# Attention in front of a mixture of experts: another order within the attention steps, and part of the first head norm on GpSimd

## The reference

```python
# x: 4 sequences of 512 tokens, 512 wide; 16 heads of 32
h = layernorm(x)
q, k, v = split(h @ w_qkv)
q, k = layernorm_per_head(rope(q)) * s + b, layernorm_per_head(rope(k)) * s + b
a = tril((q @ k.T) ** 4)
x = x + ((a / a.sum(-1)) @ v) @ w_out
h = layernorm(x)
# 16 experts in 4 groups, 2 groups and 4 experts kept; a shared expert
w, sel = route(sigmoid(h @ gate.T) + bias)
x = x + sum_over_sel(w * expert_sel(h)) + shared(h)
```

## Time and profile before

| what | us |
|---|---|
| three timed runs | 1215.68, 1217.14, 1225.99 |
| their median | 1217.14 |
| the profiled execution, its own time | 1209.58 |
| its span in the trace | 1207.6 |
| first scores of sequence 0 | 88.9 |
| sequences 0 to 3 start | 88.9, 207.7, 357.1, 496.8 |
| attention ends | 609.8 |
| PE, DVE, ACT, POOL busy over the span | 958.4, 756.9, 563.6, 529.1 |

### The profile page before, as it was taken

How to read it: one execution, slowest core, us unless ns; L and a number is a source line. 1 busy time by engine, 2 the same in 40 slices (tenths; PEclk the granted TensorE clock), 3 DMA queues, 4 the chain that set the end, 5 groups by cost and what they waited for, 6 DMA issues and landing times. The chain is left out here.

```text
span 1207.6 us, 21002 instructions
## 1 busy us (share of the span) xinstructions
PE 958.4 (79%) x5770; PEld 455.7 (38%) x5771; DVE 756.9 (63%) x1663; ACT 563.6 (47%) x1009; POOL 529.1 (44%) x738
## 2 busy tenths in 40 slices
PE   5967789869777785984777799888888798878883
PEld 2432333324333332341343454444344344434441
DVE  2857865867888588849648665554455544545552
ACT  2347874866537665577235234333333233333330
POOL 0005663544415545367302003555555555555553
PEclk9988999888879887976868899899999989999996
DMA  8002333433323333655346896777777777778874
GB/s 330 13 35 93 118 105 137 140 119 112 107 88 100 137 107 110 236 204 192 107 148 207 304 319 184 193 185 184 174 188 191 178 179 181 190 174 193 183 187 78
DMA packets 76648, 193.48 MB, mean 160 GB/s; under 512 B 9904, under 2 KB 11056, under 8 KB 75312
## 3 DMA queue, kind: packets, MB, share of 16 engines
q1 hardware_dynamic: 58672, 149.53, 35.9%
q0 software_dynamic: 17920, 43.26, 19.6%
HBM read 131.67 MB, written 61.10 MB: 160 GB/s over the span
## 5 line engine op out<-in xcount | busy, mean ns | idle before, releaser
L743 PE MATMUL bank<-arena,xgT 128*128 (+1 forms) x1152 | 288.0, 387 | 3.6 <-ACT xgT L1029 3.1
L1065 POOL TENSOR_TENSOR s_p<-s_p,c_causal 128x128 f32<-128x128 f32 x256 | 153.8, 624 | 304.3 <-DVE s_p L1420 282.7
L485 PE MATMUL bank<-arena 128*128 128x512 f32 x384 | 196.5, 663 | 43.8 <-ACT arena L856 14.6
L1022 ACT ACTIVATE hT<-bank 128x512 f16<-128x512 f16 x96 | 57.3, 597 | 273.1 <-PE bank L753 273.1
L743 PEld LDWEIGHTS bank<-arena,xgT 128*128 128x128 f16 x1152 | 109.2, 100 | 133.1 <-issue 45.4
L1073 POOL TENSOR_TENSOR arena<-arena 128x768 f16<-128x768 f32 x68 | 113.0, 1662 | 87.8 <-ACT arena L821 87.7
L1109 POOL DMA_INDIRECT out<-yy,sidx x80 | 128.6, 1608 | 46.1 <-issue 44.6
L764 PE MATMUL bank<-wd,hT 128*128 128x512 f16 x576 | 146.0, 391 | 0.7 <-ACT hT L1022 0.7
L910 ACT ACTIVATE arena<-bank 128x512 f32<-128x512 f32 (+3 forms) x256 | 100.8, 439 | 93.2 <-PE bank L533 92.6
L1694 DVE TENSOR_SCALAR yy<-bank,hsc 128x512 f32<-128x512 f32 x80 | 60.0, 750 | 122.8 <-DMA out<-yy,sidx 116.6
L1029 ACT ACTIVATE xgT<-bank 128x1024 f16<-128x1024 f16 x96 | 98.2, 1023 | 78.7 <-PE bank L734 77.4
(11 more groups left out here) (172 smaller groups left out, 1390.2 us busy)
## 6 DMA issues: line engine op xcount, KB each, us to landing
wd<-w_scratch SPq DMA_DIRECT2D x82, 512.0 KB, 4.2
arena<-w_experts SPq DMA_DIRECT2D x34, 768.0 KB, 6.0
w_scratch<-arena SPq DMA_DIRECT2D x34, 768.0 KB, 4.5
arena<-w_scratch SPq DMA_DIRECT2D x17, 1024.0 KB, 7.7
xin<-x SPq DMA_DIRECT2D x4, 1024.0 KB, 5.5
arena<-x SPq DMA_DIRECT2D x4, 1024.0 KB, 4.8
x_scratch<-arena SPq DMA_DIRECT2D x4, 1024.0 KB, 5.2
xg<-xn_scratch SPq DMA_DIRECT2D x16, 256.0 KB, 4.5
```

The costliest lines, as they stand in the source:

```text
L485: mm = pe.matmul(bk[:], xnT[:, c, m * P:m * P + P], wqkv[:, c, w * E:w * E + E], start=(c == 0), stop=(c == EC - 1))
L743: mm = pe.matmul(bank[2 + k][:], xgT[:, k, xh * EC + c, :], w, start=(c == 0 and xh + wh == 0), stop=(c == EC - 1 and xh == 1))
L1065: pool.tensor_tensor(d, d, C["causal"][:], ALU.mult).then_inc(p4_masked, 1)
```

## The change

- q/k/v stage of the first sequence: the temporaries of rope exist twice there (the second pair lies in `s_sq`), and DVE ropes block m before the variance of block m - 1. DVE stops at the reciprocal (new semaphore `rstd_known`); Pool makes the product into `qkn` and, for blocks 0 to 2, the low halves. PE and ACT have the stage written out in a new order, and the next sequence's transposes and first q and k stand ahead of the last block's transposes. The weight load is split into q/k and v (`wv_in`).
- Sequences 0 to 2: at p = 0 PE does the old group's `values` ahead of v; ACT does both casts of `qkT` at the end of the p = 3 step, the four squares together, then `copy_v` and `head_squares`; its other copies move from the head of a step to the end of the one before. DVE's `finish` moves from the head of the p = 1 step to behind the fourth powers of the p = 0 step. At i = 15 `choice_places` stands ahead of `centre`. SP stores the normed rows one expert piece earlier.
- Sequence 3: `finish` likewise; the logits come in two halves at steps 5 and 6, and the choice starts a step later, `compare` and `expert_choice` then sharing a step.

```diff
-        t1, t2 = (t12[:, 2 * i:2 * i + 2, :].rearrange("p j n -> p (j n)") for i in range(2))
+        roped = [[a[:, 2 * i:2 * i + 2, :].rearrange("p j n -> p (j n)") for i in range(2)] for a in (t12, s_sq)]
+        temps = lambda b, m: roped[m % 2 if b == 0 else 0]
...
+        rstd_known, wv_in = sem("rstd_known"), sem("wv_in")
...
-            sp.dma_start(wqkv, w_qkv).then_inc(wqkv_in, 16)
+            sp.dma_start(wqkv[:, :, 0:2 * E], w_qkv[:, :, 0:2 * E]).then_inc(wqkv_in, 16)
+            sp.dma_start(wqkv[:, :, 2 * E:3 * E], w_qkv[:, :, 2 * E:3 * E]).then_inc(wv_in, 16)
...
-                halves_of(b, 0, 2)
+                halves_of(b, 0, 1)
                 if b:
                     sp.wait_ge(xn16_ready, b)
                     sp.dma_start(xn_dram[N * (b - 1):N * b, 0:E].rearrange("(m p) e -> p m e", p=P),
                                  xn16[(b - 1) % 2].rearrange("p m h e -> p m (h e)").bitcast(I32)).then_inc(xn2_out, 16)
-                halves_of(b, 2, 4)
+                halves_of(b, 1, 4)
...
-                elif i == 5:
-                    for m in range(MB):
+                elif i in (5, 6):
+                    pe.wait_ge(x2T_sb, upto(pb, 3))
+                    for m in (2 * i - 10, 2 * i - 9):
                         logits(pb, m, bkA)
...
                     scores(b, i)
+                    if i and i % MB == 0:
+                        values(b, i - 1)
                     if b + 1 < B:
                         fill(b, i)
-                    if i:
+                    if i % MB:
                         values(b, i - 1)
...
+            def first_qk(m):
                 for w, (done, read) in enumerate(((q_ps, q_roped), (k_ps, k_roped))):
                     if m:
                         pe.wait_ge(read, upto(0, m - 1))
                     qkv(0, m, w, bank[w], done)
+
+            def first_v(m):
                 if m:
-                    if m >= 2:
-                        pe.wait_ge(qkT_sb, 2 * upto(0, m - 2))
-                    qk_transposes(0, m - 1, bank[6], bank[7])
                     pe.wait_ge(v_sb, upto(0, m - 1))
+                else:
+                    pe.wait_ge(wv_in, 16)
                 qkv(0, m, 2, bank[2], v_ps)
-            for m in range(MB):
-                pe.wait_ge(xT_sb, upto(0, m + 2) if m < 2 else upto(1, m - 2))
-                first_T(1, m, bank[4 + m % 2])
+
+            def first_qkT(m):
+                if m:
+                    pe.wait_ge(qkT_sb, 2 * upto(0, m - 1))
+                qk_transposes(0, m, bank[6], bank[7])
+
+            first_qk(0)
+            first_v(0)
+            first_qk(1)
+            pe.wait_ge(consts_in, 16 * NCST)
+            pe.wait_ge(memset_done, 1)
+            first_qkT(0)
+            first_qk(2)
+            first_v(1)
+            first_qkT(1)
+            first_qk(3)
+            first_v(2)
+            first_qkT(2)
+            first_v(3)
+            for m, bk in enumerate((bkA, bank[3], bkB, bank[3])):
+                pe.wait_ge(xT_sb, upto(0, 3) if m < 3 else upto(1, 1))
+                first_T(1, m, bk)
+            pe.wait_ge(xT_sb, upto(1, 0))
+            qkv(1, 0, 0, bkA, q_ps)
+            pe.wait_ge(xT_sb, upto(1, 2))
+            qkv(1, 0, 1, bkB, k_ps)
+            first_qkT(3)
             pe.wait_ge(xT_sb, upto(1, 3))
-            qkv(1, 0, 0, bkA, q_ps)
-            qkv(1, 0, 1, bkB, k_ps)
-            pe.wait_ge(qkT_sb, 2 * upto(0, 2))
-            qk_transposes(0, 3, bank[6], bank[7])
             for b in range(B):
                 sequence(b)
             pe.wait_ge(table_added, B - 1)
@@ -879,6 +905,7 @@
             def head_squares(b, m):
                 act.wait_ge(centred, upto(b, m))
+                t1, t2 = temps(b, m)
                 act.activation(t2, t1, ACT.Square).then_inc(squares, 1)
...
-                if p == 0 and m:
-                    qkT(nb, m - 1, bkA, bkB, (0,))
-                elif p == 1:
-                    if m:
-                        copy_v(nb, m, bkA)
-                    elif b:
-                        copy_first(nb, 3, bkA)
-                    if i == 5 and b:
-                        copy_rows(pb, 1, bkB)
-                    elif i == 9 and b:
-                        copy_logits(pb, bkB)
-                        gate_scores(pb)
-                    elif i == 13 and lb < B:
-                        copy_first(lb, 1, bkB)
-                elif i == 10:
+                if i == 3 and b:
+                    copy_rows(pb, 0, bkA)
+
+            def behind(b, i):
+
+                nb, pb, lb, m, p = b + 1, b - 1, b + 2, i // MB, i % MB
+                if p == 3:
+                    qkT(nb, m, bkA, bkB)
+                elif i == 0 and b:
+                    copy_first(nb, 3, bkA)
+                elif i == 4 and b:
+                    copy_rows(pb, 1, bkB)
+                elif i == 5 and b:
+                    copy_rows(pb, 2, bkB)
+                elif i == 6 and b:
+                    copy_rows(pb, 3, bkA)
+                elif i == 8 and b:
+                    copy_logits(pb, bkB)
+                    gate_scores(pb)
+                elif i == 9:
                     copy_v(nb, 0, bkB)
-                elif i == 3 and b:
-                    copy_rows(pb, 0, bkA)
-                elif i == 6 and b:
-                    copy_rows(pb, 2, bkB)
-                elif i == 7 and b:
-                    copy_rows(pb, 3, bkA)
-                elif i == 11 and lb < B:
+                elif i == 10 and lb < B:
                     copy_first(lb, 0, bkA)
-                elif i == 14 and lb < B:
+                elif i == 12 and lb < B:
+                    copy_first(lb, 1, bkB)
+                elif i == 13 and lb < B:
                     copy_first(lb, 2, bkB)
...
-                elif i == 6:
+                elif i == 7:
                     copy_logits(pb, bkA)
...
                     square(b, i, 1)
-                    if nb < B and p == 0:
-                        if m:
-                            qkT(nb, m - 1, bkA, bkB, (1,))
-                        head_squares(nb, m)
                     square(b, i, 2)
                     fourth(b, i, 1)
                     square(b, i, 3)
                     fourth(b, i, 3)
+                    if nb < B and p == 0:
+                        if m:
+                            copy_v(nb, m, bkA)
+                        head_squares(nb, m)
                     if i == 2 and b:
                         rows_hi(b - 1)
                     split_next(b, i)
+                    if nb < B:
+                        behind(b, i)
...
-                if nb < B:
-                    qkT(nb, 3, bkA, bkB)
...
-            for m in range(MB):
-                if m:
-                    qkT(0, m - 1, bank[6], bank[7])
-                    if m == 2:
-                        deviation(2)
-                copy_v(0, m, bank[2])
-                head_squares(0, m)
-                head_deviation(0, m)
-                if m == 2:
-                    first_norm(2, range(MB))
-            for m in range(MB):
-                copy_first(1, m, bank[4 + m % 2])
+            copy_v(0, 0, bank[2])
+            head_squares(0, 0)
+            head_deviation(0, 0)
+            qkT(0, 0, bank[6], bank[7])
+            deviation(2)
+            head_squares(0, 1)
+            head_deviation(0, 1)
+            copy_v(0, 1, bank[2])
+            first_norm(2, range(MB))
+            qkT(0, 1, bank[6], bank[7])
+            head_squares(0, 2)
+            head_deviation(0, 2)
+            copy_v(0, 2, bank[2])
+            qkT(0, 2, bank[6], bank[7])
+            copy_v(0, 3, bank[2])
+            copy_first(1, 0, bkA)
+            copy_first(1, 1, bank[3])
+            head_squares(0, 3)
+            head_deviation(0, 3)
+            copy_first(1, 2, bkB)
+            copy_first(1, 3, bank[3])
             qkT(0, 3, bank[6], bank[7])
...
+            for m in range(MB):
+                pool.wait_ge(rstd_known, m + 1)
+                if m:
+                    pool.wait_ge(qkT_ps, 2 * m)
+                    pool.wait_ge(qkT_sb, 2 * m)
+                heads = lambda a: a.rearrange("p (h d) -> p h d", d=D)
+                pool.tensor_tensor(heads(qkn[:]), heads(temps(0, m)[0]), hs[:, 2, :].unsqueeze(2).to_broadcast([P, 2 * H, D]),
+                                   ALU.mult).then_inc(qkn_ready, 1)
+                if m < MB - 1:
+                    for w, dst in enumerate((q16[0], k16[0])):
+                        pool.wait_ge(qkT_sb, 2 * upto(0, m) - 1 + w)
+                        pool.tensor_tensor(dst[:, 1, :, m * P:m * P + P], qk32[:, w, :].rearrange("p (c n) -> p c n", c=4),
+                                           dst[:, 0, :, m * P:m * P + P], ALU.subtract).then_inc(qk_lo, 1)
...
-                ps, a1, a2 = heads(src[:]), heads(t1[:, w * E:w * E + E]), heads(t2[:, w * E:w * E + E])
+                ps = heads(src[:])
+                a1, a2 = (heads(a[:, w * E:w * E + E]) for a in temps(b, m))
...
```

(46 more changed lines are left out.)

6 lines of the change are left out of this document (2 added, 4 removed).

## The result

| | before | after |
|---|---|---|
| median of the timed runs, us | 1216.9 | 1176.9 |
| ratio after/before, 95% interval | | 0.9661 [0.9627, 0.9694] |
| profiled execution, own time / span | 1209.58 / 1207.6 | 1174.85 / 1173.1 |
| first scores | 88.9 | 93.2 |
| sequences 0, 1, 2, 3 | 118.8, 149.4, 139.7, 113.0 | 108.9, 134.1, 127.9, 108.2 |

The forecast was 1193.2 (range 1177 to 1209): the direction is right, the size is not. The change gained 40.0 us by the medians, against 23.9 forecast. Medians and ratios in this document leave out three executions (one each of e10, e15 and e16) that lay over 1.5% above the fastest of their kernel.

What follows compares the result with a forecast made beforehand. Chains of waits between engines in the first 609.8 us, with no engine full, were taken as the bound. Terms -2.4 - 4.4 - 10.6 - 9.5 + 3 = -23.9 off the median 1217.14 gave 1193.2 us, range 1177 to 1209.

Steps and rivals of the forecast that it cites:

- q/k/v stage: First sequence's opening stage: scores 2.5 us earlier, third head 2.3 gained, 2.4 charged for PE's clock; net gain 2.4 us.
- sequence 0: First sequence's attention: earlier casts and copies shorten PE's waits; gain 4.4 us, bounds 0 and 11.6.
- sequences 1, 2: Middle sequences: new step order and no DMA wait gain 10.6 and 9.5 us; bounds 3 each, 19.9 and 19.4.
- sequence 3: Last sequence's attention: halved logits bring scores 6 forward 3.4 us but the choice starts 3.8 later; cost 3, bounds 0 and 5.
- expert part: Rest of the span behind 609.8 us: no line of the change lies there, so no change; over 3 us would show error.
- part 2: Step order in sequences 0 to 2: earlier casts, squares, finish and store gain 4.4, 10.6 and 9.5 us.
- The late finish: Sequences 1 and 2: finishing earlier brings PE 5 to 11 us but DVE nothing, its work being only reordered.
- Half given back: Lower bound for sequences 1 and 2: only the DMA waits go, half of that given back; 3 us each.
- Rival A: Sequences 0 to 2: waits go almost whole, PE's clock stays at 2.4 GHz; -41 us, 1176; chance 0.16.
- The loop: q/k/v stage: rope of k, variance, root, reciprocal, Pool's product, transposes, then q and k take 13.7 us a block, against 11.2.
- rival C: q/k/v stage: loop over Pool takes 18.5 us a block, kernel slower, 1221 to 1234; sign: scores behind 92; chance 0.06.
- the later choice: Sequence 3: choice of experts starts 3.8 us later, DVE has no gap from there to the last table; cost 3 us.

Runs made afterwards that it cites:

- e10: Changed kernel with DVE's finish in sequences 0 to 2 back ahead of the second step's fourth powers; ratio to the kernel before 0.9776.
- e15: The changed kernel repeated without any edit; median 1176.7 us, ratio to the kernel before 0.9679.
- e16: Repeat of e1, the changed kernel with the q/k/v stage of before; median 1172.1 us, ratio to the kernel before 0.9632.
- e18: Changed kernel with both DVE's finish and PE's values in sequences 0 to 2 put back; ratio to the kernel before 0.9847.
- e11: Changed kernel with PE's values of the old group back behind v in sequences 0 to 2; ratio to the kernel before 0.9870.
- e3: Kernel before with only SP's store of the normed rows one expert piece earlier; ratio to the kernel before 0.9847.
- e12: Changed kernel with the choice of places back behind DVE's centring at the last step; ratio to the kernel before 0.9675.
- e7: Changed kernel with ACT's order in sequences 0 to 2 put back; ratio to the kernel before 0.9888.
- e17: Changed kernel with e13's PE and ACT order in the q/k/v stage, product kept on Pool; median 1175.5 us, ratio to the kernel before 0.9666.
- e4: Kernel before with only sequence 3 changed (halved logits, later choice, finishes behind fourth powers); ratio to the kernel before 1.0008.
- e2: Kernel before with only the q/k/v stage changed; ratio to the kernel before 1.0012.
- e13: Changed kernel with q/k/v stage reordered: PE's q and k ahead of transposes, product on DVE, ACT's squares ahead of casts; ratio to the kernel before 0.9647.
- e14: e13 with DVE's zero-store wait later, next rows' statistics and ACT's block 1 casts earlier; median 1168.6 us, ratio to the kernel before 0.9620.
- e1: Changed kernel with the q/k/v stage of before; ratio to the kernel before 0.9703.

## Why the prediction was right or wrong

By the sum's own terms, against the profiles (before and after):

| term | forecast | profiles | what the runs say |
|---|---|---|---|
| q/k/v stage | -2.4 | +4.2 to the first scores | +2.9 there, +1.0 at the end of sequence 2 (e15, e16) |
| sequence 0 | -4.4 | -9.9 | 108.9 again in e15 |
| sequences 1, 2 | -10.6, -9.5 | -15.3, -11.8 | finish and values 16 of all three (e18) |
| sequence 3 | +3.0 | -4.8 | -1.4 to -1.8, the rest by the clock's level |
| expert part | 0 | +3.0 | within its scatter |

**The step that failed** is in part 2: "The late finish brings PE 5 to 11 us but DVE nothing, because its work is the same in another order", with the values ahead of v priced at "0.6 of each wait". Measured by e10, e11 and e18 this one edit is worth 16 us. The reason I gave is true of a DVE that is full, and the windows said that it was busy 78% of sequences 1 and 2. The finish is short, 2.6 us from its first transpose to the end of its product in e11, but it held the banks that PE needed, and behind PE's values stood the scores that ACT and DVE needed next (e10); with the finish early and the values late, DVE stood before the finish instead (e11). I followed DVE's own list of work and not the circle through PE. The rest of the gain of sequences 0 to 2 (the kernel before at 408 to 414 in three profiles, e18 at 387.1) is 21 to 27 us for the store, ACT's order and the places together, and that is what I had forecast for the whole part, 24.5. That the two agree is partly luck: the whole was priced with an edit worth 16 in it at nothing, and sequence 0 gave 9.9 where 4.4 was forecast.

**What held.** The DMA wait that goes with the earlier store, and the direction of all of part 2. "Half given back" as the lower bound for the store was too low: e3 gained nearly twice the wait. The choice of places is small, 4 us by the one profile of e12 and nothing by its ratio. Rival A had nearly the right sizes for the sequences (7, 14.5, 14.5) and the right total, 1176. Its direction is what e7 and e10 show: the waits of DVE do hang on PE and ACT standing still, not on DVE being full. Its reasons were only half right, and its total was in part luck. DVE's waits for squares fell by half, not by three quarters; the granted clock rose (0.97, 0.91 and 0.89 for 0.94, 0.85 and 0.87), but PE's busy time in sequences 0 to 2 did not fall; and A's 5 us for the stage and nothing for sequence 3 were 4.2 lost and 4.8 gained.

**The stage** was right in mechanism and wrong in size. The loop goes as I wrote it, rope of k, variance, root, reciprocal, product, transposes, q and k; it measured 15.8 and 14.9 instead of 13.7 twice. The first scores, 93.2, came behind the 92 that I had set as the sign of rival C; C's loop of 18.5 us didn't come. (C's 14.4 us count the loop three times where my sum holds it twice, with one more product and v behind it; at C's prices that is some 13.) The first product took 2.93 (I had 2.1; later ones took 1.91), the transposes behind it 1.7 instead of 1.23, and PE's q and k after an idle of 6.49 us 7.6 instead of 6.98. The first reciprocal ended at 40.8, not 37.4: the first rope was 1.4 later, and PE took 8.83 us for the 16 instructions of block 1's q and k, at a granted clock of 0.81, so that DVE waited 2.04 for k. The first fourth power of the third head came 2.4 us closer behind the scores, as forecast (2.3): it is the second of two that start at 97.14 and end at 98.42, 4.6 behind the scores where the earlier trace rows has 7.0. It bought little: sequence 0 is 0.3 us shorter in e15 than in e16. That trade-off was never good: 2.43 us of DVE's work were bought with a loop through three engines, while DVE's 11.2 a block stood beside PE's own 11.7.

The rule of the Trainium skill that I had weighed there (GPSIMD Engine Reference, 4.1 Engine selection) says about twice as slow; the traces have 1.91 on Pool against 1.23 on DVE, 1.6 times, and my line had 2.1. By e17 it is the loop and not Pool that costs.

**Sequence 3.** The forecast counted the halved logits at the lower level, as in the earlier trace rows, and charged the later choice 3 us. In the profile of after they ran at the upper level, 4.24 us in two parts for 7.01. e4, at the lower level, is still 2.2 shorter than before, so the charge was wrong as well: DVE's gap of 10.43 became two of 4.45 and 4.12 in the changed kernel.

**The base.** I took the gain off the median but argued from one execution, and sequences 0 and 1 of that one were 1 to 3 us shorter each than the same code in e2 and e4. That is the side on which the 5.3 us lie that the profiles lack of the medians' gain. One trace doesn't tell it.

## What to carry to other kernels

Ask of a short instruction what it holds (a bank, a buffer), not how long it takes, and follow the circle until it comes back to the engine you started from: a finish of 2.6 us was worth 16 because PE's next scores stood behind it. Edits of order come in sets: ACT's order and the store alone gave 0.5 and 1.5%, the whole 3.4%, and only undoing one at a time from the finished kernel shows what each carries. Work moved to a slower, idle engine pays only where its result isn't on the way to the next instruction of the engine that is the bound; with the loop cut the first scores came 4 to 6 us earlier (e17, e13), with the start freed as well 10 (e14), where moving the work had cost 3 to 4. e14 has the lowest median, 1168.6, but its interval overlaps those of e15 and e16. Last, time the same program twice before reading a small difference between two ratios: e1 and e16, one program, came out 0.7% apart.
